# Squaring the attention scores in two 512-wide ScalarE instructions, and loading Wv with a cast instead of from a scratch copy

## What is computed

```python
xn = _layernorm(x)
# attention branch: 16 query heads of width 128, 8 key/value heads
q, k, v = xn @ Wq, xn @ Wk, xn @ Wv
logG = cumsum(log_sigmoid(6.906768 + xn @ Wg))          # per key/value head
a = ((q . k) / sqrt(128)) ** 2 * exp(logG[t] - logG[s])  # causal, s <= t
y = (a @ v) / (sum(a) + 1e-6)
s = y @ Wc + bc
# feed-forward branch
h = silu((xn @ gate_w.T) * gate_s) * ((xn @ up_w.T) * up_s)
g = silu((h @ down_w.T) * down_s)
x = x + s * g
```

## Time and profile before

| what | us |
|---|---|
| runs of the kernel before | 8818.81 and 8743.64, median 8781.23 |
| the profiled execution, its own time | 7883.43 |
| its span on the slowest core (core 7) | 7881.8 |
| the spans of the eight cores | 7844.9 to 7881.8 |

### The profile page before, as it was taken

The page is one execution under the profiler, slowest core; times in us unless marked ns, Lnnn a source line. Parts: engine busy times, 40 slices in busy tenths (PEclk is TensorE's granted clock), DMA queues, the critical chain, the costliest instruction groups (busy, mean ns, idle before and its releaser), DMA issues.

```text
span 7881.8 us, 107956 instructions; the slowest of 8 cores (7844.9 to 7881.8 us)
## 1 busy us (share of the span) xinstructions
PE 6774.8 (86%) x43624; PEld 3401.2 (43%) x43624; DVE 994.5 (13%) x2180; ACT 2004.6 (25%) x2296; POOL 558.0 (7%) x1190
## 2 busy tenths in 40 slices
PE   4999998668999997767999998777699999977777
PEld 2444444324444444433444444554344443455553
DVE  1000011321000011122000011111300000110002
ACT  2121011311120013531111011665122100156661
POOL 0000000100000000100000000000000000000000
PEclk9999999789999998888999999888899999999998
DMA  5444342063444441034444343101534444310004
GB/s 118 76 75 76 69 91 52 14 153 83 75 76 72 67 91 38 23 75 125 78 76 75 67 93 60 25 18 30 160 65 76 78 70 84 71 41 23 23 12 129
DMA packets 248460, 552.62 MB, mean 70 GB/s; under 512 B 103905, under 2 KB 120417, under 8 KB 240289
## 3 DMA queue, kind: packets, MB, share of 16 engines
q0 software_dynamic: 96944, 365.00, 26.4%
q1 hardware_dynamic: 132594, 147.15, 6.2%
q10 hardware_dynamic: 18432, 33.56, 1.7%
HBM read 855.92 MB, written 54.53 MB: 116 GB/s over the span
## 4 chain that ended last, share of the span: by engine, by line
PE 63%; ACT 13%; DMA 10%; DVE 7%; issue 4%; POOL 2%; ACTq 1%; DVEq 0%; SPq 0%; POOLq 0%
PE pball L430 31%; PE pball L484 15%; ACT a2p L742 11%; PE pball L656 4%; PE pball L775 3%; PE pball L594 3%; DMA x<-x 3%; DVE a2p L822 2%; PE pball L569 2%; DMA out<-x 2%; POOL a2p L751 2%; PE pball L726 2%; PE pball L886 1%; DMA ar<-wq 1%; DMA ar<-wk 1%
## 5 line engine op out<-in xcount | busy, mean ns | idle before, releaser
L430 PE MATMUL pball<-ar 128*128 128x512 bf16 x11264 | 2442.1, 380 | 5.2 <-DVE ar L306 5.2
L430 PEld LDWEIGHTS pball<-ar 128*128 128x128 bf16 x11264 | 1104.2, 98 | 1341.6 <-issue 19.1
L742 ACT ACTIVATE a2p<-pball,sc_tok 128x1024 bf16<-128x1024 f32 (+3 forms) x1152 | 1201.8, 1043 | 1344.6 <-PE pball L726 644.3
L484 PE MATMUL pball<-ar 128*128 128x512 bf16 x5632 | 1266.5, 386 | 89.9 <-DVE scrA L498 83.4
L775 PE MATMUL pball<-ar,a2p 128*128 128x128 bf16 x8448 | 914.0, 225 | 204.0 <-DVE ar L847 105.0
L775 PEld LDWEIGHTS pball<-ar,a2p 128*128 128x128 bf16 x8448 | 783.5, 104 | 400.0 <-issue 315.2
L726 PE MATMUL pball<-ar 128*128 128x512 bf16 x2304 | 748.5, 414 | 182.2 <-ACT a2p L742 176.7
L484 PEld LDWEIGHTS pball<-ar 128*128 128x128 bf16 x5632 | 556.7, 99 | 799.0 <-issue 163.2
L782 PE MATMUL pball<-ones_col,a2p 128*128 128x1 bf16 x8448 | 847.8, 171 | 0.0
L782 PEld LDWEIGHTS pball<-ones_col,a2p 128*128 128x128 bf16 x8448 | 736.0, 98 | 120.9 <-issue 34.1
L441 ACT ACTIVATE a2p<-pball,gsc_s 128x512 bf16<-128x512 f32 x352 | 241.9, 687 | 1866.6 <-PE pball L430 1828.9
(11 more groups left out here) (92 smaller groups left out, 2263.4 us busy)
## 6 DMA issues: line engine op xcount, KB each, us to landing
ar<-gw POOLq DMA_DIRECT2D x176, 512.0 KB, 5.5
ar<-uw POOLq DMA_DIRECT2D x176, 512.0 KB, 7.5
ar<-dw POOLq DMA_DIRECT2D x176, 512.0 KB, 5.1
ar<-wq POOLq DMA_DIRECT2D x64, 512.0 KB, 5.2
x<-x ACTq DMA_DIRECT2D x128, 256.0 KB, 3.6
ar<-wc POOLq DMA_DIRECT2D x16, 2048.0 KB, 15.6
out<-x SPq DMA_DIRECT2D x128, 256.0 KB, 3.1
x_buf<-x SPq DMA_DIRECT2D x16, 1024.0 KB, 6.7
```

The source lines that it names most:

```text
L430: b.op("tensor", lambda e, half=half, cg=cg, ts=ts, bank=bank, slot=slot: e.matmul(pb[bank][:, 0:512], gu_sl(slot, half, cg), xnT_sl(cg, t ...
L484: b.op("tensor", lambda e, ic=ic, tc=tc, slot=slot: e.matmul(pb[tc][:, 0:512], hdn_sl(ic, tc * 128, 128), dn_sl(slot, ic % 4), start=(ic = ...
L742: b.op("scalar", lambda e, src=src, dst=dst, j=j, jh=jh: e.activation(dst, src, AF.Square, scale=sc_tok[:, j * 8 + jh:j * 8 + jh + 1]), ma ...
```

## The change

Two parts.

**Squares.** The ACTIVATE of `emit_sq`, which took both heads (two PSUM banks) at once, becomes two, one per head. The first waits for the scores and for its own half of the buffer, the second for the other half. `sq_done[j]`, for which the next scores, the products with V and POOL wait, stays one value: that of the second.

**Wv.** The bf16 scratch copy `wv_bf` is gone, and with it `wv_tmp`, the two loads, the two stores and the three waits at the start. In each block Wv is loaded from the f32 original with a cast, by POOL instead of SP, at the same place in the program text.

```diff
-            for vh in range(2):
-                b.dma("gpsimd", g_wv,
-                      wv_tmp[:, :, :], wv_d[:, :, vh * 512:vh * 512 + 512],
-                      waits=[(s_wv, s_wv.n)])
-                b.dma("sync", s_wv, wvb_d[:, :, vh * 512:vh * 512 + 512],
-                      wv_tmp[:, :, :], waits=[(g_wv, g_wv.n)])
-            wrdy["wvb"] = (s_wv, s_wv.n)
-            for eng in ("vector", "scalar", "gpsimd"):
-                b.wait(eng, s_wv, s_wv.n)
...
-                    b.dma("sync", s_wv, wv_st, wvb_d,
-                          waits=[(tm, s3_done), wrdy["wvb"]])
-                    wv_rdy = (s_wv, s_wv.n)
+                    b.dma("gpsimd", g_wv, wv_st, wv_d, waits=[(tm, s3_done)])
+                    wv_rdy = (g_wv, g_wv.n)
...
-                                src = pball[:, jp * 1024:jp * 1024 + 1024].rearrange(
-                                    "p (h t) -> p h t", h=2)[:, :, c0:512]
-                                dst = a2p[jp].rearrange("p (h t) -> p h t", h=2)[:, :, c0:512]
-                                w = [(tm, qk_marks[j]), a2_free[jp * 2],
-                                     a2_free[jp * 2 + 1], (vm, gate_vm[0])]
-                                b.op("scalar", lambda e, src=src, dst=dst, j=j, jh=jh: e.activation(
-                                    dst, src, AF.Square,
-                                    scale=sc_tok[:, j * 8 + jh:j * 8 + jh + 1]),
-                                    mark=sm, waits=w)
+                                scol = sc_tok[:, j * 8 + jh:j * 8 + jh + 1]
+                                for hi in range(2):
+                                    src = pb[jp * 2 + hi][:, c0:512]
+                                    dst = a2[jp * 2 + hi][:, c0:512]
+                                    w = [(tm, qk_marks[j]), a2_free[jp * 2 + hi],
+                                         (vm, gate_vm[0])]
+                                    b.op("scalar", lambda e, src=src, dst=dst, scol=scol: e.activation(
+                                        dst, src, AF.Square, scale=scol),
+                                        mark=sm, waits=w)
```

More of the change, by code:

```diff
@@ L145, in build @@
     out_d = nc.dram_tensor("out", [T, C], F32, kind="ExternalOutput").ap()
-    wvb_d = nc.dram_tensor("wv_bf", [128, NCG, HK * 128], BF16).ap()
     ksc_d = nc.dram_tensor("k_sc", [HK, 128, T], BF16).ap()
@@ L168, in build @@
         s_g64 = b.sem("s_g64")
-        s_wv = b.sem("s_wv")
         s_bc = b.sem("s_bc")
@@ L217, in build, with emit_init @@
         wrdy = {}
-        def emit_init(ds_row, wv_tmp):
+        def emit_init(ds_row):
             b.dma("sync", s_misc, idbf[:, :], idbf_d)
@@ L932, in emit_phase2 @@
                     scr2_free[0] = (vm, vm.n)
-                for s in s_x + s_x2 + s_kb + s_vb + s_ke + s_ve + [s_g64, s_wv, s_misc]:
+                for s in s_x + s_x2 + s_kb + s_vb + s_ke + s_ve + [s_g64, s_misc]:
                     b.wait("sync", s, s.n)
@@ L939, in emit_phase2 @@
                 b.flush()
-        with nc.sbuf_tensor("ds_row", [1, C], F32) as _dsrow, \
-                nc.sbuf_tensor("wv_tmp", [128, NCG, 512], BF16) as _wvtmp:
-            emit_init(_dsrow, _wvtmp)
+        with nc.sbuf_tensor("ds_row", [1, C], F32) as _dsrow:
+            emit_init(_dsrow)
         emit_phase2()
```

## The result

| what | before | after |
|---|---|---|
| median of the runs | 8555.69 (10 runs, 7885.48 to 8818.81) | 8362.67 (11 runs, 8171.63 to 9029.13) |
| the profiled execution | 7883.43 | 8173.03 |
| span of its slowest core | 7881.8 (core 7) | 8171.2 (core 5) |

The changed kernel is slower, by a ratio of **1.0354, interval 1.033 to 1.0378**. The medians alone would tell the opposite: eight more runs of the kernel before brought its median from 8781 down to 8555.69, and its lowest to 7885.48. In the profiled executions the change costs 8173.03 - 7883.43 = 289.6 us; the sum said 313.

The account below looks back on a forecast made before the run. Inside attention's units ACT was taken as the bound, one square after the other. The terms 268 + 20 + 73 - 48 = +313 us, added to the runs' median 8781, gave 9094, range 8950 to 9240.

Parts of the forecast that it names:

- the sum: Whole kernel: squares 268, ends of units 20, Wv in the blocks 73, start -48, together +313 us.
- The base: Runs' median 8781, 898 above the profiled execution; the terms, called unstretched by a lower PE clock, were added to it.
- Squares: Attention: one square of 1024 becomes two of 512, step 1.73 for 1.37, +0.355 us each; 268 us plus 20 at ends.
- 756 steps that pay: Attention: 756 intervals inside units, over eight heads and S = 8 to 32, each 0.355 us dearer, 268 us.
- the sum had 20: Ends of attention units: narrow squares become pairs too, 0.35 us net in each of 56 units, 20 us.
- Wv in the blocks: K projections: wk tiles land behind Wv, which takes 25 us; PE waits 20 a block, 18 net, +73 us in all.
- the 8 us for a K projection at half clock: K projections: some 2 us more in each block because K begins at half clock after the wait.
- Start: Kernel start: first x load issued at 4.7 instead of 51.33, layer norm begins at 16 to 20; -48 us.
- Rival 1: Attention: PE-bound at half clock in the runs, step 1.92 hides the pair; total 8806; chance 0.10.
- Rival 2: Attention squares: second half starts without its 0.15 gap, step 1.58; total 8973; chance 0.08.
- Rival 3: K projections: the software queue serves tiles beside Wv, K starts on time; total 9004; chance 0.10.
- Rival 4: Attention: PE's clock falls inside units as PE works 1.1 of 1.73 instead of 1.37; step 1.92; chance 0.10.

Follow-up runs that it names:

- experiment 6: Kernel before with one wait per square and Wv loaded with a cast in eight pieces between wk tiles; run twice: core 7 7801.5, then lowest 7793.93, ratio 0.9888.
- experiment 2: Changed kernel with repeated waits ahead of squares folded: lowest 8136.95; changed kernel with second half not waiting for ACT's own previous instruction: lowest 7951.82, ratio 1.0057.
- Experiments 1: Kernel before with only the squares split: 8139.44; kernel before with only the Wv part of the change: lowest run 7906.53.
- Experiment 4: Kernel before with Wv cast by POOL, issued behind two wk tiles: core 7 took 7860.5; the same with Wv in eight pieces between tiles: 7840.28, ratio 0.9963.

## Why the prediction was right in the mechanism and wrong in the time

- **The base failed.** The step was the last one of the sum: "The runs' median is 8781, 898 above it, and no row says why; ... so I add them as they are". The 898 is no property of the kernel. Both runs of that median were far above what the kernel needs: ten runs of it have a median of 8555.69 and a lowest of 7885.48, beside the profiled execution. The 9094 and the whole range, 8950 to 9240, stood on it; the time is 8362.67, below it. A range that took in a base anywhere between 7883 and 8781 would have held the time. That a lower PE clock does not stretch the squares is what the runs show: in the profile of the second kernel of experiment 6 a square took 1.114 on core 7, at a mean clock of 0.900, and 1.113 on core 0, at 0.933. The gap of the up scaling behind the gate scaling, with one wait in it, was 0.096 and 0.095. That it does not stretch the DMA terms no run shows: with folded waits (experiment 2) Wv took 25.7 on core 4, at 0.880, and 22.9 on core 0, at 0.920, and in the changed kernel 23.3 to 30.6 on core 5 alone.
- **The ratio: luck in part.** The forecast's own ratio, 9094/8781 = 1.036, is inside the measured interval, 1.033 to 1.0378. But its difference was 23 too large (313 for 289.6) and its base 898 too large, and the two errors cancel. On the right base the same 313 give 8196/7883 = 1.040, above the interval.
- **Squares: right in mechanism and per step, not in the count.** 687 ns twice, gaps of 0.20 and 0.15, steps of 1.72, block 3 at 939 for 932; attention is 281 longer for 288. Experiments 1 and 2 show the cause; folding waits shows the price of one, and dropping the own wait shows what the second half's gap is. But the prediction counted 756 steps that pay. ACT's timeline before the change has only 653 distances of 1.35 to 1.40 between full squares (core 7; 708 with those from a full to a narrower one), and after it 712 of 1.68 to 1.78, counted in the second way (core 5); 653 x 0.355 is 232. The other 50 lie in the ends of units and in the longer half clock between them, for which the sum had 20. That the total came out is luck in part.
- **Wv in the blocks: right in the mechanism, with two sizes off.** Wv took 25.8 for 25. The new waits are 90.7 and not 4 x 20 = 80, because in block 0 Wv itself took 30.6 and PE waited 26.14. Against it, the 8 us for a K projection at half clock did not come: its matmuls are 2.4 us longer in all (232.5 for 230.1). So +73 was met by +76. Experiment 4 shows that the order on the queue makes the wait.
- **Start: the sum right, its working not.** -48.4 for -48. But the x load was issued at 5.43 and not 4.7, its landing took 15.9 where it had taken 13.6, and layer norm began at 21.36, outside the 16 to 20 that were given: 43.6 sooner. "Behind it is layer norm, unchanged" was wrong too, as its stop of 5.84 for x went away. The two errors cancel.
- **Not in the sum:** the output projections are 15 us shorter on the chain (core 5 against core 7) and 18 in the mean over the cores. The last table of the experiments shows that this comes with the split squares; how, stays open. It and some 8 of the squares are what is missing from 313.
- **Rival 1** (PE-bound attention): fell, the ratio is not 1.0. **Rival 2** (no gap): fell for this kernel, but its mechanism is real: dropping the own wait makes it, even to an overlap of 0.10. **Rival 3** (tiles served beside Wv): refuted by 26.14 and by the moved wait. **Rival 4** (clock falls in the units): refuted as it was put, since the granted clock is 1.00 inside the units with 0.51 idle in each step (before it was 0.15 a step by the earlier trace rows, not the 0.3 written there). The upper end of the range, 9240, took in its time; no run shows the term behind it, a step of 1.92 at a clock that falls inside the unit: 1.72 was measured, at 1.00. But the clock does play a part that no rival had: it stays at half for about 180 us more, between units. At 1.92 a step that is some 95 steps which take 1.92 and not 1.73, about 18 us, an estimate.

## What to carry to other kernels

Take a change's cost as a ratio to the time of the execution that was profiled, and give an absolute time only as wide as the spread of its base. Count what stands between two instructions of a busy engine: here the split cost 0.355 a step, and 0.25 of them went away with the second half's wait for the first. When a sum comes out, check its terms one by one: here three of them were met by errors that cancel. Before expecting time from a faster link, add up the ring of waits through all engines and divide by its buffers (here 2.61 by two pairs, 1.30 a step); and where a queue serves its loads in order, as POOL's did here, put a large load behind, or between, the small ones that are needed first (waits for `wk` of 90.7 with Wv ahead, 29.6 with it behind two tiles, 6.8 with it in pieces).

## What the runs showed of the hardware that was not expected

- Two squares overlapped by 0.10 us even with a wait for PE between them, whose value has been reached (experiment 2, all 960 full pairs). A wait for the first of them turned that into a gap of 0.15 in the changed kernel: 0.25 for one wait instruction.
- A further wait instruction ahead of a square cost 0.055 here even when its value had been reached. The gaps are 0.093 with the own wait alone, 0.148 with one more, 0.203 with two more (changed kernel) and 0.26 with three more (kernel before); with one folded away the step went from 1.72 to 1.67.
- With ACT no longer late, the two squares of a pair of buffers ran together and then both stood, so that the timeline of ACT alone looked idle by 0.41 in 2.61, and that of PE by 0.31: neither engine was full and the step could still not be shorter.
- With longer idle times of PE in each step (0.51 for 0.15) its granted clock stayed at 1.00 inside a unit, but between two units it was at half for some 13 us where it had been some 7.
